# Sixteen-wide heads: in even slots the scores go ahead of the first transpose of probabilities

## What is computed

```
x = x + L0_attn(norm(x))            # 32 heads of 16, signs of weights
x = x + L0_xattn(norm(x), ctx)      # 32 heads of 128
x = x + L0_ffn(norm(x))
x = x + L1_attn(norm(x))            # 32 heads of 16, one k and v, causal, alibi
x = x + L1_xattn(norm(x), ctx, ctx) # 32 heads of 16
x = x + L1_ffn(norm(x))             # experts
# an attention with heads of 16:
scores = einsum('bhqd,bhkd->bhqk', q, k) / sqrt(16)
attn   = softmax(scores [+ table or mask])
out    = einsum('bhqk,bhkd->bhqd', attn, v) @ Wo
```

## Time and profile before

| | us |
|---|---|
| median of 3 runs | 2214.37 (2214.03 to 2215.72) |
| profiled execution, its own time | 2216.86 |
| its span, first to last instruction | 2215.1 |
| TensorE busy | 2128.2 (96%) |
| VectorE busy | 1345.6 (61%) |
| ScalarE busy | 1041.8 (47%) |
| GpSimdE busy | 902.8 (41%) |
| mean granted TensorE clock | 0.99 |

### The profile page before, as it was taken

How to read it: one execution, slowest core, us unless ns; L and a number is a source line. 1 busy time by engine, 2 the same in 40 slices (tenths; PEclk the granted TensorE clock), 3 DMA queues, 4 the chain that set the end, 5 groups by cost and what they waited for, 6 DMA issues and landing times. The chain is left out here.

```text
span 2215.1 us, 45113 instructions
## 1 busy us (share of the span) xinstructions
PE 2128.2 (96%) x18734; PEld 1725.6 (78%) x18734; DVE 1345.6 (61%) x2350; ACT 1041.8 (47%) x1778; POOL 902.8 (41%) x675
## 2 busy tenths in 40 slices
PE   6996999999999999999999999999999999999998
PEld 4674888888887888888888877888888777777766
DVE  6885644443444354444344558797786788888866
ACT  5775553544535555354553552111112767777632
POOL 2687232331414414143231345121122668878611
PEclk8998999999999999999999999999999999999999
DMA  4000111011111101111111113000001100100002
GB/s 168 2 21 1 59 39 58 22 38 44 37 55 58 52 26 39 58 39 42 37 39 36 43 52 112 0 0 0 0 1 59 39 2 16 50 27 11 2 1 76
DMA packets 23054, 81.01 MB, mean 37 GB/s; under 512 B 4048, under 2 KB 6224, under 8 KB 16720
## 3 DMA queue, kind: packets, MB, share of 16 engines
q1 hardware_dynamic: 22864, 78.28, 10.3%
HBM read 74.08 MB, written 4.19 MB: 35 GB/s over the span
## 5 line engine op out<-in xcount | busy, mean ns | idle before, releaser
L2620 PE MATMUL xat_TP<-shared_rounded 128*128 128x512 f32 x1024 | 321.5, 395 | 0.1
L2292 POOL TENSOR_TENSOR xat_T<-xat_T,xat_mask 128x512 f32<-128x512 f32 x64 | 82.0, 1294 | 478.9 <-DVE xat_T L2382 478.9
L104 PE MATMUL xat_G<-xat_xnT_hi,shared_rounded 128*128 128x512 f32 x768 | 244.5, 391 | 0.0
L2279 POOL TENSOR_TENSOR shared_rounded<-shared_landing,shared_rounded 128x2048 fp32r<-128x2048 f32 x39 | 179.5, 4611 | 152.4 <-ACT shared_rounded L2136 152.4
L2620 PEld LDWEIGHTS xat_TP<-shared_rounded 128*128 128x128 f32 x1024 | 188.3, 188 | 44.6 <-issue 6.2
L2620 PE MATMUL xat_TP<-shared_rounded,xat_oT_lo 128*128 128x512 f32 x512 | 199.8, 390 | 0.0
L2373 DVE RECIPROCAL xat_q_inv_rms<-xat_OT 128x16 f32<-128x16 f32 x32 | 8.3, 258 | 304.5 <-PE xat_OT L2545 304.5
L104 PE MATMUL ffn_H<-shared_rounded 128*128 128x448 f32 (+1 forms) x816 | 179.1, 368 | 3.7 <-DVE ffn_h_kept L1445 2.4
L1377 POOL TENSOR_TENSOR ffn_one_hot<-ffn_one_hot,ffn_block_rank 128x448 f32<-128x448 f32 x64 | 75.4, 1178 | 253.9 <-DVE ffn_one_hot L1426 253.9
L1353 ACT ACTIVATE shared_rounded<-ffn_TP 128x384 fp32r<-128x384 f32 x64 | 34.9, 545 | 293.3 <-PE ffn_Y L1502 246.4
L104 PEld LDWEIGHTS ffn_H<-shared_rounded 128*128 128x128 f32 x816 | 152.3, 188 | 21.3 <-DVE ffn_h_kept L1445 5.0
(11 more groups left out here) (362 smaller groups left out, 4978.5 us busy)
## 6 DMA issues: line engine op xcount, KB each, us to landing
shared_landing<-in_Cq_q SPq DMA_DIRECT2D x16, 1024.0 KB, 4.9
shared_landing<-in_Cq_o SPq DMA_DIRECT2D x16, 1024.0 KB, 4.7
shared_landing<-in_Cq_kv SPq DMA_DIRECT2D x8, 1024.0 KB, 7.3
shared_landing<-in_ctxT_paired SPq DMA_DIRECT2D x4, 1024.0 KB, 7.2
two_ctxT_raw<-in_ctxT SPq DMA_DIRECT2D x8, 512.0 KB, 4.0
shared_landing<-in_w1T SPq DMA_DIRECT2D x8, 448.0 KB, 4.0
shared_landing<-in_w SPq DMA_DIRECT2D x7, 512.0 KB, 3.6
out<-X SPq DMA_DIRECT2D x6, 512.0 KB, 3.0
```

The costliest lines, as they stand in the source:

```text
L104: last = eng.matmul(out, a, b, start=(n == 0), stop=(n == len(steps) - 1))
L2279: return eng.tensor_tensor(w[1][:, :, :], landed[:, :, :], w[0][:, :, :].bitcast(F32), ALU.subtract)
L2292: eng.tensor_tensor(T[:, n, :, :], T[:, n, :, :], mask[:, :].unsqueeze(1).to_broadcast([P, ROWS, SEQ]), ALU.add)\
L2620: last = eng.matmul(TP[m % 2][:, :], x, w, start=(n == 0), stop=(n == len(steps) - 1))
```

## The change

In even slots TensorE's queue has the scores first and the first turn second. No instruction is added or removed, and the order on the other engines stays. Odd slots stay as they are.

```
             for s in range(SLOTS):
+                if s < LASTP and s % 2 == 0:
+                    scores(s)
                 if LAG <= s < LASTP + LAG:
                     turn(2 * (s - LAG))
-                if s < LASTP and s % 2 == 0:
-                    scores(s)
                 if LAG + 2 <= s < LASTP + LAG + 2 and s % 2 == 1:
                     values((s - LAG - 2) // 2)
```

## The result

| | before | after |
|---|---|---|
| median, us | 2214.2 (2211.01 to 2215.72) | 2233.69 (2231.48 to 2234.36) |
| ratio, 95% interval | | 1.0081 (1.0069 to 1.0093) |
| profiled execution, its own time | 2216.86 | 2231.48 |
| its span | 2215.1 | 2229.7 |
| TensorE's waits for the copies of TP, stage two | 4.1 x8 | 20.9 x29 |

What follows compares the result with a forecast made beforehand. TensorE was taken to bound stage two, with gqa mixed. Stage two +18.1, gqa up to slot 24 +4.2 and its last group -4.5 made +17.8; 2216.9 + 17.8, less 2.5, gave 2232.2 us, range 2224 (2221 with some absorption) to 2241.

Steps and rivals of the forecast that it cites:

- slot 40: Stage two, position 0: S fills T1's 0.89 us wait for ScalarE and product y hides T2, -1.0 us.
- part 1: Bare even slots: T2 waits for C1, +0.88 us each or 0.6; stage two 5.3 at position 4, 3.7 at position 2.
- Part 2: Stage two, position 0, x transposes after T2: +1.0 us in each of six slots, 6.0; slot 40 the reverse, -1.0.
- T3 + 1.0: Position 0 of stage two: C1, exponentials and C2 run later, so T3 starts +1.0 us later than before.
- absorbed: Rival: earlier S ends all 14.2 us of stage two's older TensorE waits; +3.6 us in all, 2218 us; chance 0.07.
- Part 3: Stage two, position 6: C2 is late behind ScalarE's queue and delays T3, +0.72 us in four slots, together 4.1.
- Part 4: Gqa up to slot 24, ten even slots: the same terms as in stage two, sum +4.2 us.
- Part 5: Gqa's last group: S fills T1's 1.48 us wait; 34.3 us instead of 38.84, so -4.5, some 3.8 of it clock.
- a pair takes 8.3: Gqa's last group: a pair of slots takes 8.3 us instead of 10.07, as VectorE's own ring has less than that.
- The assumption that the clock holds: Gqa's last group: the clock stays up in the new order; if it falls as before, 3.9 us comes back.
- VectorE been the ring: Rival: VectorE sets the pace, all 44 even slots gain 0.53 us, 23 us in all, 2191 us; chance 0.05.
- rule on cycling through PSUM: Rival: new 0.78 us holes lower stage two's clock, 1.29 us a slot, 26 us in 20 slots, 2258; chance 0.06.

Runs made afterwards that it cites:

- the kernel with slot 40 as well: Kernel before, with scores first only in slots 26, 28 and 30 of gqa and slot 40 of stage two: 2210.9 against 2216.66 us, ratio 0.9973.
- the kernel with the filler transposes: Kernel before, with eight extra identity transposes ahead of T1 in slots 26, 28 and 30 of gqa: 2216.53 against 2216.66 us, ratio 1.0.

## Why the prediction was right, and where its terms were not

| term | predicted | traces of the whole change | alone |
|---|---|---|---|
| bare slots, positions 2 and 4 | 9.0 | 10.5 | 10.5 |
| position 0, six slots | 6.0 | 2.5 | 2.4 |
| slot 40 | -1.0 | -0.8 | -0.7 |
| position 6 | 4.1 | 4.8 | 5.1 |
| gqa up to slot 24 | 4.2 | 3.6 | 3.5 (timed 4.7) |
| gqa's last group | -4.5 | -3.5 | -2.2 (timed -2.0) |
| sum | 17.8 | 17.1 | 18.6 |

**What bounds it, and part 1: right.** TensorE is the bound of stage two, C1 is the cost, and the hole is the 0.78 us of the drain. The slots at full price cost 0.92 to 0.96 and not 0.88, and those where C1 had been late 0.67 to 0.72, not 0.6. At position 2 a few of the small ones were 0.32 to 0.36 rather than 0.15. The slot at position 4 that was put at nothing, slot 60, cost 0.18. Together 1.5 us short.

**Part 2: the mis-sized term.** "T3 + 1.0" was right; "none of it is won back behind" was wrong. Slot 16 of the changed kernel, against the earlier trace rows:

```profile
1818.45 1.14 ACT L595 ACTIVATE two_T<-two_T 128x512 f32<-128x512 f32 x2
...
1819.97 1.08 ACT L237 ACTIVATE shared_rounded<-two_G 128x512 fp32r<-128x512 f32 x2
1820.23 0.63 PE L1084 MATMUL two_TP<-ident,two_T 128*128 128x128 f32 x4
1820.60 1.29 DVE L243 TENSOR_TENSOR shared_rounded<-two_G,shared_rounded 128x512 fp32r<-128x512 f32 x2 [0.76 <-ACT shared_rounded L237]
...
1821.79 3.02 PE L104 MATMUL two_G<-two_Wo,shared_rounded 128*128 128x512 f32 x12
...
1826.28 0.66 PE L225 MATMUL two_G<-ident,shared_landing 128*128 128x128 f32 x4 [0.60 <-DVE X L883]
```

Two rows of the kernel before, from its slot 17, that answer to the last two:

```profile
1819.40 3.06 PE L104 MATMUL two_G<-two_Wo,shared_rounded 128*128 128x512 f32 x12 [0.17 <-DVE shared_rounded L243]
...
1824.33 0.66 PE L225 MATMUL two_G<-ident,shared_landing 128*128 128x128 f32 x4 [0.99 <-DVE X L883]
```

From the start of the x copies to that of the low halves were 1.31 us before and are 0.63 now. Before, the low halves stood behind VectorE's own addition and maxima, after their data had come; now VectorE waits for the data. So they are late by 1.0 less that 0.7. I had carried ScalarE's delay on to VectorE as if VectorE had no slack there. From T3 to the product y were 1.80 us and are 1.56, from y to the last x transposes 4.93 and are 4.49: of 1.0 late, 0.24 and 0.44 are won back, and 0.3 to 0.4 stays. This is the rival "absorbed" in small, in six slots: of the earlier trace rows the wait for X gave back 2.6 us and the low halves 2.3, not all 14.2.

**Part 3: right**, 0.83 a slot where 0.72 was worked out; the experiment with the exponentials behind C2 shows its cause.

**Part 4: near**, with position 0 over-sized and slots 12, 14 and 20 under-sized (0.9, 0.7 and 0.87, not 0.75, 0.56 and 0.5). Slots 8 and 10 together cost 0.33 and slots 16 and 18 together 0.13, where 1.0 was stated for each two. In both kernels S of slots 10 and 18 waits 0.30 to 0.34 us for VectorE's subtraction, so VectorE sets the pace there and swallows most of what the copy costs in the slot before.

**Part 5: the right sign, too large a size.** T1 of slots 26 to 30 now starts at 170.76, 179.29 and 188.37, so the pairs take 8.3, 8.5 and 9.1 us. The step that failed is "a pair takes 8.3": it took the 1.48 us wait out and asked of VectorE's ring alone what comes next. It was GpSimdE. The rows of slot 30 of gqa in the changed kernel:

```profile
186.15 1.21 PE L1073 MATMUL gqa_S<-gqa_Kbd,gqa_qT 32*64 32x128 f32 x64
...
187.26 2.06 POOL L727 TENSOR_TENSOR gqa_T<-gqa_T,gqa_row_inv 128x512 f32<-128x512 f32 x2
...
188.37 0.66 PE L1084 MATMUL gqa_TP<-ident,gqa_T 128*128 128x128 f32 x4 [1.01 <-POOL gqa_T L727]
```

GpSimdE ends the first of the two multiplications just before T1 at 188.37; ahead of it in its queue are three operations of 1.27 us each for the sums of the group before. The window of this group has GpSimdE busy 41.8 of 49 us, the highest share of any engine, and 41.5 of 52 stood already in the earlier trace rows. I read VectorE's 67% there and passed over GpSimdE's 80%. The assumption that the clock holds was not sure either: it held to 196.6 us in this trace, and the same order with gqa alone lost it once, at 190.7 us, and took 36.91 us for the group.

**The rivals did not come true.** Had VectorE been the ring, even slots would have become shorter; of the 29 steps between even slots of stage two only those from slots 38 and 40 did. The older waits absorbed 4.9 us and not 14.2. The granted clock of stage two is 1.00 with 20.9 us of waits for the copies in 29 holes. The Trainium skill's rule on cycling through PSUM (TensorE: Matmul & The Clock Gate, "A second HAM failure mode: psum-queue depth-cycling") would have lowered it by such holes; no run here shows that.

**Luck.** The errors have both signs: 3.5 us too many at position 0, 2.2 too few in bare and v slots, 1.0 too much gain in gqa. The sum is nearer than its terms: 0.7 us off by the traces. That 2232.2 lies within 1.5 us of the median is luck as well, since the kernel's medians of before alone moved by more than 2 us from round to round.

## What to carry to other kernels

With one buffer between two turns, what stands between them on TensorE is the cover of the copy; moving it out costs the idle time of that round trip, which a drain of the same kernel shows directly. When a delay is passed from one engine to the next, subtract first how long the next one's instruction stood in its own queue after its data had come. And reorder only where the trace shows the instruction waiting: the same swap that lost 0.8% everywhere gained 0.27% (0.16 to 0.37) in the four slots where T1 had been late, though three of the four alone gained 0.09%, which is not told from nothing.

## What the runs showed of the hardware that I had not expected

The clock in gqa does not follow from the order of the instructions alone. The same wait of T1 for L727 in slot 28, 1.12 us long, stands in the traces of two kernels with the same order in gqa:

```profile
178.83 0.66 PE L1084 MATMUL gqa_TP<-ident,gqa_T 128*128 128x128 f32 x4 [1.12 <-POOL gqa_T L727]
180.26 0.63 PE L1084 MATMUL gqa_TP<-ident,gqa_T 128*128 128x128 f32 x4 [0.78 <-ACT gqa_PT L601]
182.56 0.60 PE L1084 MATMUL gqa_TP<-ident,gqa_T 128*128 128x128 f32 x4
```

is the kernel with slot 40 as well, where the clock held at 2.4 GHz until 195.7 us; and

```profile
176.46 0.66 PE L1084 MATMUL gqa_TP<-ident,gqa_T 128*128 128x128 f32 x4 [1.12 <-POOL gqa_T L727]
177.90 0.63 PE L1084 MATMUL gqa_TP<-ident,gqa_T 128*128 128x128 f32 x4 [0.78 <-ACT gqa_PT L601]
181.54 0.85 PE L1084 MATMUL gqa_TP<-ident,gqa_T 128*128 128x128 f32 x4
```

is the kernel with the last group alone, where it stood at 1.2 GHz from 178.6 to 182.0 us and T2 to T3 took 3.64 us and not 2.30. A wait of 1.69 us left the clock up in the kernel with the filler transposes, while one of 1.48 us was followed by a fall in the kernel before and in the changed one at 196.6 us. The same order in gqa thus lost the clock once or not at all in the group's middle, and the opening of the kernel differs in the same way. Up to slot 4 of gqa all fourteen kernels have the same order, and their traces take 51.8 to 52.1 us with 3.4 us at half clock in it, 52.5 to 53.6 with 6.8, 54.0 to 54.8 with 10.2 and 55.0 to 55.3 with 13.6. A gain of a few us that rests on the clock has to be timed in many runs; a single trace, mine in the prediction included, can't give its size.
